# Joining the opening of a two-layer transformer kernel with its first attention: values projected at once, keys in two buffers

## The reference

```python
mod = (_silu(L0_c) @ L0_wmod).reshape(...)          # sa, ca, ga, sb, cb, gb
ga, gb = sign * max(abs, 0.25)
h = _layernorm(x) * (1 + ca) + sa
x = x + ga * attention0(h)                          # 16 heads, 4 key/value groups, head size 128,
                                                    # rotary positions, causal mask
h = _layernorm(x) * (1 + cb) + sb
x = x + gb * ffn0(h)                                # 256 -> 1024 -> 256, 2 of each 4 kept
# layer 1: the same frame around attention1 (4 heads, 2 groups) and a mixture of experts
```

## Time and profile before

| what | before |
|---|---|
| median of 3 runs | 824.6 us (823.23 to 826.42) |
| profiled execution, its own time | 822.92 us |
| its span in the profile | 821.1 us |
| instructions in the trace | 13589 |
| TensorE / its weight loads busy | 744.0 us (91%) / 639.5 us (78%) |
| VectorE / ScalarE / GpSimd busy | 576.0 (70%) / 461.0 (56%) / 355.7 us (43%) |
| mean granted TensorE clock | 0.976 of full |

### The profile page before, as it was taken

One profiled execution on the slowest core, in us unless ns is written; L12 is line 12 of the kernel. 1 busy time (PEld: TensorE's weight loads), 2 busy tenths in 40 slices (PEclk: granted clock), 3 DMA queues, 4 the chain that ended last, 5 costly groups with the idle time before them and its releaser, 6 DMA issues. The chain is left out here.

```text
span 821.1 us, 13589 instructions
## 1 busy us (share of the span) xinstructions
PE 744.0 (91%) x4560; PEld 639.5 (78%) x4560; DVE 576.0 (70%) x1314; ACT 461.0 (56%) x931; POOL 355.7 (43%) x374
## 2 busy tenths in 40 slices
PE   4969999999998999999998887997898999889997
PEld 2558888788887888888887776997776778666787
DVE  3735767666767576775677679897758887856667
ACT  2446666646666466664666543332558776737442
POOL 1193675417654365544444215000354554403874
PEclk9978999999999999999999998998999999999999
DMA  7250000000000000000000000000500000000001
GB/s 281 73 165 7 14 17 17 14 7 15 7 27 8 13 6 13 7 13 14 8 1 14 2 1 1 1 1 1 155 0 1 1 1 1 1 1 2 2 1 52
DMA packets 19868, 19.83 MB, mean 24 GB/s; under 512 B 2142, under 2 KB 18014, under 8 KB 19806
## 3 DMA queue, kind: packets, MB, share of 16 engines
q1 hardware_dynamic: 18478, 17.88, 7.0%
q10 hardware_dynamic: 1328, 1.18, 0.4%
HBM read 18.01 MB, written 1.05 MB: 23 GB/s over the span
## 5 line engine op out<-in xcount | busy, mean ns | idle before, releaser
L978 POOL TENSOR_TENSOR at_swapped<-at_swapped,at_sin 128x512 f32<-128x512 f32 x40 | 51.6, 1291 | 174.9 <-ACT at_swapped L758 174.9
L793 ACT ACTIVATE at_probs<-at_probs,at_negmax 128x128 f32<-128x128 f32 (+7 forms) x128 | 99.5, 777 | 28.2 <-DVE at_negmax L872 24.7
L872 DVE CUSTOM_DVE_ANT_0 at_probs<-at_scores,causal 128x128 f32<-128x128 f32 (+7 forms) x128 | 96.3, 752 | 22.3 <-PE at_scores L675 19.5
L686 PE MATMUL at_turn<-ident_sb,at_probs 128*128 128x128 f32 x576 | 85.5, 276 | 12.1 <-DVE at_full_T_lo L887 11.2
L686 PEld LDWEIGHTS at_turn<-ident_sb,at_probs 128*128 128x128 f32 x576 | 66.8, 141 | 20.7 <-issue 6.6
L673 PE MATMUL at_scores<-at_kT_hi,room 128*128 128x512 f32 (+1 forms) x192 | 67.9, 354 | 10.2 <-POOL room L1000 5.2
L785 ACT ACTIVATE at_edge_T_hi<-at_turn 128x128 fp32r<-128x128 f32 (+3 forms) x128 | 55.6, 434 | 37.5 <-PE at_turn L686 37.1
L674 PE MATMUL at_scores<-at_kT_lo,room 128*128 128x512 f32 (+1 forms) x192 | 67.5, 352 | 0.0
L675 PE MATMUL at_scores<-at_kT_hi,room 128*128 128x512 f32 (+1 forms) x192 | 67.3, 351 | 0.0
L785 ACT ACTIVATE at_full_T_hi<-at_turn 128x512 fp32r<-128x512 f32 x64 | 38.4, 599 | 49.4 <-PE at_turn L686 47.7
L887 DVE TENSOR_TENSOR at_edge_T_lo<-at_turn,at_edge_T_hi 128x128 fp32r<-128x128 f32 (+3 forms) x128 | 61.3, 479 | 1.3 <-ACT at_edge_T_hi L785 1.3
(11 more groups left out here) (377 smaller groups left out, 2418.4 us busy)
## 6 DMA issues: line engine op xcount, KB each, us to landing
at_wq_in<-L_attn_Wqkv SPq DMA_DIRECT2D x16, 128.0 KB, 2.2
at_wo_in<-L_attn_Wo SPq DMA_DIRECT2D x16, 128.0 KB, 2.0
staging<-L_ffn_routed_w SPq DMA_DIRECT2D x7, 256.0 KB, 4.7
wmod<-L_wmod SPq DMA_DIRECT2D x3, 512.0 KB, 7.6
wmod<-L_wmod SPq DMA_DIRECT2D x1, 1536.0 KB, 11.4
x<-L_attn_x ACTq DMA_DIRECT2D x1, 1024.0 KB, 5.8
at_wkv_in<-L_attn_Wqkv SPq DMA_DIRECT2D x8, 128.0 KB, 4.9
staging<-L_ffn_w_gate SPq DMA_DIRECT2D x1, 1024.0 KB, 5.3
```

The lines of the kernel that those rows point to most:

```text
L686: mm = pe.transpose(p_turn[t % 2][:, b - b0, :], probs[:, s % 4, b * P:(b + 1) * P], m.ident[:, :])
L793: act.activation(row, row, ACT.Exp, scale=-1.0, bias=negmax[:, s % 4:s % 4 + 1], accum_out=rowsum[:, s // NT % 2, i:i + 1])\
L872: dve.tensor_tensor_reduce(out=probs[:, s % 4, 0:width], in0=p_scores[s % 2][:, 0:width], in1=m.causal[:, S - width:], scale=-1.0, scalar= ...
L978: pool.tensor_tensor(swapped[:, b, :], swapped[:, b, :], sin[:, cols], ALU.mult).then_inc(rope_turned, 1)
```

## The change

- `opening` is gone; its work for layer 0 stands in the main block of `attention0`, in another order. x is loaded in two halves by two queues. The loads come in order of use, with only the first 512 columns of `L0_wmod` before the first key and query weights. Columns of the modulation are computed directly by matmuls with one moving column (`mod_columns`) and no longer by transposing rows. Only the two gates remain as rows (`gate_rows`). GpSimd spreads the condition vector and normalizes four of the eight tiles. VectorE forms the gates in unit 5 of head 0, where before it was done ahead of splitting `hT`. The second columns stand ahead of VectorE's first cosine product.
- Values of all four groups are projected at once: eight jobs of six matmuls of 512 columns, the first four ahead of unit 0, the other four in units 0 to 3 of head 0. They are kept in `values`, which lies over `staging` and `staging1`.
- So the FFN weights are loaded only once the third group's last product with its values is made (`att_mm`), and layer 1's attention weights in FFN 0.
- `kT` has two buffers. GpSimd makes the high and low parts of keys as of queries; `k_next`, `keys_hi` and `keys_lo` go.
- The modulation of layer 1 moves to FFN 0: TensorE in units 5 and 6, ScalarE reads it, GpSimd forms the gates at the end. Its 1.5 MB are loaded at the block's start.
- The loop over groups is unrolled and the `nop` instructions ahead of some GpSimd and VectorE operations are gone. Three warming matmuls stand in the opening, where before five ended it.

```diff
-        opening(nc, a, m, sems, sb, load_early, split_early)
-        kT, v = pair("kT", [P, S]), pair("v", [P, NT, D0])
-        k_next = buf("k_next", [P, S])
+        kT = [pair(f"kT{n}", [P, S]) for n in range(2)]
+        values = nc.alloc_sbuf_tensor_at("at0_v", [P, KV0, 2, NT, D0], F32R, offset=m.staging_at)
+        value_banks = score_banks + [p_proj[:, :], p_att[:, :]] * 2
...
             @block.sync
+                sp.dma_start(m.x[:, 0:4, :], a["L0_attn_x"].rearrange("o (n p) d -> p (o n) d", p=P)[:, 0:4, :]).then_inc(x_in[0], 16)
+                for n in range(2):
+                    sp.dma_start(craw[:, n, :], a[f"L{n}_c"]).then_inc(c_in, 16)
+                sp.dma_start(wmod[:, :, 0:BANK], w_rows[:, :, 0:BANK]).then_inc(wmod_in[0], 16)
+                load_k(0)
+                load_q(0)
+                sp.dma_start(wmod[:, :, BANK:], w_rows[:, :, BANK:]).then_inc(wmod_in[1], 16)
+                for c in range(CH):
+                    cols = slice(c * BANK, (c + 1) * BANK)
+                    sp.dma_start(cos[:, cols], a["cos"][:, cols]).then_inc(tables_in[c], 16)
+                    sp.dma_start(sin[:, cols], a["sin"][:, cols]).then_inc(tables_in[c], 16)
+                    if c == 0:
+                        sp.dma_start(wv_in[:, :, :], wqkv[:, :, (H0 + KV0) * P:]).then_inc(wv_loaded, 16)
+                load_q(1)
...
+                        if (g, h) == (KV0 - 1, 1):
+                            sp.wait_ge(att_mm, 2 * PER_KV * (KV0 - 1))
+                            for n, name in enumerate(("L0_ffn_w_gate", "L0_ffn_w_up")):
...
             @block.tensor
+                def value_job(t):
+                    if t == 0:
+                        pe.wait_ge(wv_ready, 1)
...
+                    for k in range(KD):
+                        mm = product(pe, value_banks[t], m.hT[:, k, t * P:(t + 1) * P], wv[:, k, :], k == 0, k == KD - 1)
...
+                mod_columns(0)
+                keep_warm(pe, early_banks[1], wmod[:, 0, :], 3)
+                pe.wait_ge(const_in, 32)
+                turn_x(0)
+                turn_x(1)
+                gate_rows()
+                turn_x(2)
+                turn_x(3)
+                key_job(0, 0, early_banks[0])
+                query_job(0, 0, early_banks[1])
+                pe.wait_ge(rows_read, 1)
+                mod_columns(6)
+                key_job(0, 1, early_banks[2])
+                pe.wait_ge(col_done, 2)
+                query_job(0, 1, early_banks[3])
+                for t in range(4):
+                    value_job(t)
+                for here in slots:
+                    slot(*here)
...
             @block.vector
+                variances(dve, m, chain, range(NT))
+                columns(1)
+                inverse_roots(dve, m, chain, range(NT), 1)
+                dve.nop(nofuse=True).then_inc(rstd_done, 1)
+                for n in range(NT):
+                    if n not in POOL_TILES:
...
+                for n in range(4):
+                    split_rows(n)
+                columns(2)
+                dve.wait_ge(tables_in[0], 32)
+                cos_rope(0, 0, early_banks[0], proj_free)
+                cos_rope(1, 0, early_banks[1], query_free)
...
             @block.gpsimd
+                split_k(0)
+                split_q(0)
+                pool.wait_ge(rstd_done, 1)
+                for n in POOL_TILES:
...
+                pool.wait_ge(wv_loaded, 16)
+                split_weights(wv_in[:, :, :], wv, wv_ready)
+                pool.wait_ge(tables_in[0], 32)
+                key_turn(0, 0)
+                query_turn(0, 0)
+                split_q(1)
+                pool.wait_ge(tables_in[1], 32)
+                key_turn(0, 1)
+                query_turn(0, 1)
...
 # ffn0, tensor
+                    for half in range(2):
+                        at = (2, 5)[half] * DM if n else half * DM
+                        for k in range(KD):
+                            mm = pe.matmul(mods[n][:, half * DM:(half + 1) * DM], cwide[:, k, :], wmod[:, k, at:at + DM], start=(k == 0), stop=(k == KD - 1))
...
+                    if u == UNITS - 3:
+                        mod_rows(0)
+                    elif u == UNITS - 2:
+                        mod_rows(1)
+                        mod_columns()
...
 # ffn0, gpsimd
+                pool.wait_ge(mod_read, 3)
+                for n in range(2):
+                    out = m.gate[:, 1, n, :]
+                    chain.run(pool.tensor_scalar(sgn[:, :], out, 0.0, 2.0, ALU.is_ge, ALU.mult))
...
+                    chain.run(pool.tensor_tensor(out, out, sgn[:, :], ALU.mult))
```

More of the change, by code:

```diff
@@ L526, in blocks @@
             return [(0, min(i + 1, 4))] + ([(4, i + 1)] if i >= 4 else [])
-        QUERY_UNITS = (0, 1)
-        KEY_SLOTS, VALUE_SLOTS = [(1, 1), (2, 1)], [(0, 3), (0, 5)]
-        USES = [(h, i, kind) for h in range(PER_KV) for i in range(NT) for kind, here in (
-            ("query", i in QUERY_UNITS), ("value", (h, i) in VALUE_SLOTS), ("key", (h, i) in KEY_SLOTS), ("out", i >= 4)) if here]
-        def before(h, i, kind, first, last, kinds):
-            done = USES[:USES.index((h, i, kind))]
-            if first:
-                done = [u for u in done if not (u[2] == "out" and u[0] == 0)]
-            if last:
-                done = [u for u in done if u[2] != "key" and not (u[2] == "query" and u[0] == PER_KV - 1)]
-            return len([u for u in done if u[2] in kinds])
@@ L546, in job @@
-        def job(g, h, i, kind, first, last):
-            return g * JOBS + (2 if first else -2) + before(h, i, kind, first, last, ("value", "key", "out"))
-        def query(g, h, c):
-            return g * QUERIES + 2 + 2 * h + c
-        def rope(h, i, kind, last):
-            return 4 + before(h, i, kind, False, last, ("query", "key"))
-        def body(g, first, last, slot):
-            for s in range(UNITS):
-                slot(g, s, first, last)
-        def groups(engine, slot):
-            body(0, True, False, slot)
-            with engine.Fori(1, KV0 - 1) as g:
-                body(g, False, False, slot)
-            body(KV0 - 1, False, True, slot)
+        QUERY_UNITS, KEY_SLOTS, KEY_SPLIT = (0, 1), [(1, 1), (2, 1)], (0, 5)
@@ new lines, in attention0, with query_here, key_here, out_here @@
+        POOL_TILES = (2, 3, 6, 7)
+        slots = [(g, h, i) for g in range(KV0) for h in range(PER_KV) for i in range(NT)]
+        last_head = (KV0 - 1, PER_KV - 1)
+        def query_here(g, h, i):
+            return i in QUERY_UNITS and (g, h) != last_head
+        def key_here(g, h, i):
+            return (h, i) in KEY_SLOTS and g < KV0 - 1
+        def out_here(g, h, i):
+            return i >= 4 and (g, h) != (0, 0)
+        ropes = [("key", 0, 0), ("query", 0, 0), ("key", 0, 1), ("query", 0, 1)]
@@ new lines, in attention0 @@
+        uses = [("key", 0, 0), ("key", 0, 1)]
+        for g, h, i in slots:
+            if query_here(g, h, i):
+                ropes.append(("query", g * PER_KV + h + 1, i))
+            if key_here(g, h, i):
+                ropes.append(("key", g + 1, h - 1))
+                uses.append(("key", g + 1, h - 1))
+            if out_here(g, h, i):
+                uses.append(("out", g * PER_KV + h - 1, i - 4))
+        rope_number = {r: n for n, r in enumerate(ropes)}
+        use_number = {u: n for n, u in enumerate(uses)}
@@ L668, in scores @@
-                    if not (first and s < 2):
-                        pe.wait_ge(max_done, g * UNITS + s - 1)
+                    if i in (0, 4):
+                        pe.wait_ge(rope_done, max(rope_number["key", g, i // 4], rope_number["query", head, i // 4]) + 1)
+                    if i in (4, 5) and (g, h) != last_head:
+                        pe.wait_ge(query_free, 2 * (head + 1) + i - 4 + 1)
+                    if unit >= 2:
+                        pe.wait_ge(max_done, unit - 1)
+                    else:
+                        pe.wait_ge(v_lo, 2 * unit + 1)
@@ L956, in _ @@
+                probs_lo(KV0 * UNITS - 1)
                 last_inverse_sums(0)
```

933 lines of the change are left out of this document (423 added, 510 removed).

## The result

The changed kernel takes 796.4 us (median; 793.5 to 798.5), the kernel before 824.4 beside it: a ratio of 0.9646, with a 95% interval of 0.9626 to 0.9666. 28 us were gained where 36.4 were forecast, inside the range of 778 to 803. The profiled execution took 796.95 us around a span of 795.1, so the spans differ by 26.0 us. The forecast span was 784.7, so the span is missed by 10.4 us and the time by some 8.

A forecast was written before the change was run, and what follows sets the result against it. TensorE was taken to bound the steady heads, VectorE, GpSimd and waits the opening. Span: 821.1 - 17.5 - 4.9 - 16.5 + 2.5 = 784.7 us; adding 1.8 and 1.7 gave 788, range 778 to 803.

The forecast's parts named there:

- Part 1: First attention: projecting all values at once removes two value jobs from groups 1 to 3's first heads, gaining 17.5 us.
- the lower bound of 4.2 us: Value jobs' cost per group, read as the difference of TensorE's busy time between two stretches; 12.7 us for three groups.
- Rival 2: First attention: value jobs were cover, and without them VectorE and ScalarE waits appear; 794 us, chance 0.13.
- Part 2: Group boundaries in the first attention: double-buffered keys remove the scores' wait for the low part, gaining 4.9 us.
- The upper figure of 7.0: Upper end for double-buffered keys: at most 2.3 us at each of three group boundaries, against 3.4 us of seen waits.
- Part 3: Opening and first head: the reordered opening lets head 1 start at 60.1 us, gaining 16.5 us, between 9 and 22.
- The second half of the term: The way from the four ropes' end to head 1's start: 18.5 us, between 16 and 22, where before 21.9.
- Rival 1: Opening gains little: late first cosine product, slow clock or GpSimd's longer chain give back all but 5 us; 800, chance 0.12.
- Part 4: First FFN: taking in the second layer's modulation loses 2.5 us, between 0 and 6.
- Rival 3: First FFN's tail: GpSimd holds up VectorE, to the 6 us bound; 791.5 us, chance 0.07.
- Rivals 4 and 5: Full-clock opening gains 22, boundaries 7: 780 us (0.12); or TensorE's clock stays at half through first heads: 834 (0.04).
- the signs of being wrong: TensorE awaiting low parts every head; cosine product past 27 us; half clock beyond 70; VectorE scalings above 1 in FFN's end.

The follow-up runs named there:

- e9: Changed kernel plus two reader-less jobs of 24 TensorE matmuls, both behind unit 3's scores in the first head of groups 1 to 3: 812.1 us.
- e3: Changed kernel with the value weights' split moved off GpSimd, high part on ScalarE and low part on VectorE: 792.8 us.
- e4: Changed kernel with VectorE normalizing all eight tiles and GpSimd none: 792.15 us.
- e2: Changed kernel with VectorE's first two cosine products placed ahead of the second modulation columns: 792.4 us.
- e8: Changed kernel with the edits of e2 and e4, and head 0's gate arithmetic in two halves at units 5 and 12: 793.8 us.
- e1: Changed kernel with layer 0's ten gate operations moved from unit 5 of head 0 to behind VectorE's second cosine product: 794.8 us.
- e7: Changed kernel with layer 1's modulation products moved from units 5 and 6 of FFN 0 to between its last down products: 793.4 us.
- e6: Changed kernel without GpSimd's ten operations on the second layer's gates at the end of FFN 0: 794.6 us.
- e5: Changed kernel plus two reader-less jobs of 24 TensorE matmuls, after unit 3's and before unit 5's scores, first head of groups 1 to 3: 820.1 us.

## Why the prediction was right, and where it was off

**Part 1 (17.5 forecast).** Right in kind, too small by some 4 us: three such heads gained 21.5. The reading that failed is that the two value jobs are the only difference between a group's first head and its second; the first also lacks a query half. e9 shows TensorE's time at 5.3 us a group, 16.0 for three. This is more than the lower bound of 4.2 us, which compared stretches with different query work. Some 1.0 us more in each head were waits, and 0.9 stay open. Rival 2, that the values were cover for other work, is out: no head of groups 1 to 3 grew when they went.

**Part 2 (4.9).** The wait of the scores for the low part is gone, as told. But the last heads before a boundary gained 3.2 us in three, not 4.9. The upper figure of 7.0 (2.3 in each of three) still held the query half ahead of the boundary's scores, which stays: without its 1.37 us it is 2.9, close to what was gained. Both parts together gave 23.2 us, with the loss of 2.15 in head 1 already taken off.

**Part 3 (16.5; 9 to 22).** This failed: 7.15 us, below its range. The mechanism stood, the size did not. The step was "That gives the end of the cosine product at 22.5 us, between 20 and 27": it was 29.7. Of the 7.2 us between them 6.8 lie ahead of the columns: the split of `hT` was to end near 18.5 us and ended at 25.3. Normalization started at 13.2 us instead of 11.3, because VectorE waited 1.91 us for the first columns. It took 5.0 us, where I had halved it by giving four tiles to GpSimd at VectorE's price. And I had put the value weights' split under cover, without asking which VectorE instruction lies beside it; e3 and e4 show the casts at 0.42 us once it doesn't. The way from there to the end of the cosine product was 4.4 us, and the sum had 4.0 for it. So the second columns, with their 3.4 us of idle time, were priced about right; e2 shows that this wait could be had out. Of the 7.2 us that were missing, e2 alone gave 3.0, e4 alone 3.8, both together (e8) 5.4, each against one execution of the changed kernel, with the spread of 2.6 us told above. What is left, about 2 us, I did not separate. Two things of the trace that the sum left out lie in it. The first one-column products took 3.57 us, where the second eight took 1.84; the table by stretches gives a granted clock of 1.00 there, so the cause stays open. And the three warming matmuls behind them hold TensorE until 16.5 us, ahead of its first transpose. No run took either away.

The second half of the term, "I take 18.5 us, between 16 and 22", had 21.0. The terms that the text names for it add to 22.0 (21.9 - 5.1 - 1.3 + 2.8 + 3.7), and no reason was given for going below. Its value job of 5.1 us isn't what its row says either: 11 matmuls in 2.0 us make 4.4 for 24. The gates were in it with their 3.7 us of VectorE time. What the text left out is what the block does next: TensorE runs dry, and the clock is at 0.50 for the start of head 1. With half of the gates at unit 5 the way was 18.5 us in e8, with none of them there 17.8 in e1.

Rival 1 (a gain of 5 in the opening, 800 us, 0.12) describes this part better than my forecast. Of the mechanisms that it names the slow clock was one, with some 1.5 us in the first key and query job; GpSimd's chain of ropes took what was forecast.

**Part 4 (2.5; 0 to 6).** Measured 4.4, and for another reason than the one that I had priced highest. I gave TensorE's products 0.25 us for 256 columns. A plain float32 matmul has two records in the trace, which I had counted as two matmuls. It takes 0.43 to 0.47 us: 8 records in 1.89. The same misreading is in Part 3's bound for the one-column products. From the first start to the start of what follows, the three groups of products take 1.5, 1.7 and 1.7 us, 5.0 in all instead of about 3.5, of which the wait of the earlier trace rows covers 2.2, and 2.93 us show in the steps. e7 gives exactly this back. Rival 3, GpSimd's contention, for which I had kept the 6 us bound, is shown false by e6. The stretching is real (2.20 us for 1.43) and costs nothing, because TensorE is late there anyway. Of the rest, 0.7 us lie in the step from unit 1 to 2, which varied between 8.6 and 11.1 us over these kernels with the place where the clock fell. About 1.0 us behind the last product stays unexplained; e6 has it too, so it isn't the gate chain.

Rivals 4 and 5 did not occur. At the start of head 1 the clock stayed low for about 6 us and not for heads. Two of the signs of being wrong did: the cosine product ended later than 27 us, and the clock was low beyond 70 us (0.74 from 72 to 76).

## What to carry to other kernels

Work that is moved to a second engine has that engine's price, and it has the price of what it then lies beside; look up both for each operation on both sides. When VectorE feeds TensorE unit by unit, a block on it can cost more than its length, since TensorE runs dry and the next unit starts at the lower clock: here heads 0 and 1 took 6.2 us less in e1, without the block of 4.0. Split such a block only into slots in which the trace shows the other engine idle slot by slot, and not head by head. A stretched row is no loss until the step that it stands in gets longer: measure the step, not the row.

## What the runs showed of the hardware

- GpSimd scaled a 128x256 float32 tile by two per-partition scalars in 1.25 us. VectorE took 0.33 to 0.38 for the same, and GpSimd itself 0.40 with two constants and multiplications (the split of `wq`). Its chain in FFN 0 shows 1.07 to 1.13 us where a comparison or a maximum is in it, and 0.45 to 0.65 for a multiply and an add.
- VectorE's gate operations grew from 0.3 or 0.4 us to as much as 1.5 beside GpSimd's rope operations of 1.3 us, and ten of them from 4.0 to 10.7 us.
- A one-column plain product took 0.23 us at the full clock (8 products, 16 records, 1.84 us), about as much as a matmul of 512 columns in the split format (0.229).
- The granted clock fell behind stretches in which TensorE was busy only a part of the time (1.80 of 4 us from 20 to 24 and 1.13 from 64 to 68 us in the changed kernel, 0.92 from 80 to 84 in e8), and once, in e5, behind a wait of only 1.3 us in a head that was otherwise full. Waits of that length left it at 1.00 elsewhere, as the 1.48 us of the changed kernel's transposes at 148.97 us.
